# One ScalarE copy for the raw attention outputs of two groups

## What is computed

```python
# attention: 32 query heads of 16 dimensions, 8 key/value groups (4 heads each), 256 queries x 256 keys
score = einsum('bhqd,bhkd->bhqk', qh, kh) / sqrt(16)
attn  = softmax(score)
out   = einsum('bhqk,bhkd->bhqd', attn, vh)
x     = x + out @ Wfc.T + bfc
# then: layernorm, a router (2 of 8 experts), the routed experts and a shared one, added to x
```

## Time and profile before

| | |
|---|---|
| three runs | 790.33, 792.49 and 793.11 us; median 792.49 us |
| the profiled execution | 793.74 us, its span 792.0 us, granted TensorE clock 0.994 |
| attention in it | first exponential at 102.4 us, last copy of a raw result at 294.0 us |
| the even-group copies of groups 4 to 62 | first at 119.28 us, last at 289.67 us |

### The profile page before, as it was taken

The page is one execution under the profiler, slowest core; times in us unless marked ns, Lnnn a source line. Parts: engine busy times, 40 slices in busy tenths (PEclk is TensorE's granted clock), DMA queues, the critical chain, the costliest instruction groups (busy, mean ns, idle before and its releaser), DMA issues.

```text
span 792.0 us, 16078 instructions
## 1 busy us (share of the span) xinstructions
PE 760.2 (96%) x5151; PEld 406.6 (51%) x5152; DVE 576.0 (73%) x1194; ACT 429.7 (54%) x843; POOL 269.5 (34%) x224
## 2 busy tenths in 40 slices
PE   6998989999999988999999999999999999999897
PEld 4553533433433334556655656555555555555554
DVE  5767779999999966788789887555555555546767
ACT  3665579999999973455443553434343343323231
POOL 3362007999993301564300101111111111015431
PEclk9999989999999999999999999999999999999999
DMA  9997846556545788898588576877777777569985
GB/s 337 338 391 237 249 145 211 182 162 200 192 122 167 242 323 303 307 333 306 187 226 215 145 172 141 188 175 177 176 177 179 177 185 173 124 164 288 278 238 160
DMA packets 161782, 172.07 MB, mean 217 GB/s; under 512 B 103680, under 2 KB 117504, under 8 KB 161216
## 3 DMA queue, kind: packets, MB, share of 16 engines
q1 hardware_dynamic: 150012, 128.89, 55.8%
q0 software_dynamic: 11120, 41.43, 16.9%
q10 hardware_dynamic: 596, 1.07, 0.4%
HBM read 105.40 MB, written 42.73 MB: 187 GB/s over the span
## 4 chain that ended last, share of the span: by engine, by line
PE 76%; DVE 9%; DMA 7%; ACT 3%; issue 2%; SPq 2%; DVEq 0%; ACTq 0%
PE psum L1465 29%; PE psum L1477 15%; PE psum L1315 8%; PE psum L1301 6%; PE psum L1229 4%; PE psum L1401 4%; PE psum L1205 4%; DMA sb_weights<-attn_dram 3%; PE psum L1332 2%; ACT sb_weights L1025 1%; PE psum L1181 1%; DMA sb_hT<-sb_h 1%; DVE sb_weights L1747 1%; DMA sb_weights<-in_ctxT 1%; DMA sb_weights<-k_parts 1%
## 5 line engine op out<-in xcount | busy, mean ns | idle before, releaser
L1465 PE MATMUL psum<-sb_weights,sb_rows 128*128 (+1 forms) x1608 | 250.8, 313 | 0.6 <-DMA sb_rows<-xnT_dram 0.6
L1465 PEld LDWEIGHTS psum<-sb_weights,sb_rows 128*128 128x128 f16 x1608 | 157.3, 98 | 91.9 <-DMA sb_rows<-xnT_dram 1.1
L1025 ACT ACTIVATE sb_weights<-psum,sb_rows 128x512 f32<-128x512 f32 x256 | 158.6, 684 | 17.2 <-PE psum L1301 15.4
L1697 DVE TENSOR_REDUCE sb_rows<-psum 128x4 f32<-128x1024 f32 x128 | 150.1, 1214 | 6.1 <-PE psum L1229 6.1
L1477 PE MATMUL psum<-sb_weights,sb_hT 128*128 (+1 forms) x630 | 147.4, 379 | 2.5 <-DMA sb_hT<-sb_h 2.5
L894 POOL DMA_INDIRECT sb_rows<-xn_rows,sb_slot_tok x39 | 38.4, 984 | 217.9 <-DVE sb_rows L2286 147.8
L1477 PEld LDWEIGHTS psum<-sb_weights,sb_hT 128*128 128x128 f16 x630 | 61.3, 98 | 68.0 <-DMA sb_hT<-sb_h 3.7
L1301 PE MATMUL psum<-sb_weights 50*128 50x512 f16 x256 | 90.1, 391 | 3.0 <-ACT sb_weights L1025 2.6
L1094 ACT ACTIVATE psum<-psum 128x352 f32<-128x352 f32 x71 | 31.8, 448 | 112.2 <-DVE psum L1947 112.2
L1315 PE MATMUL psum<-sb_weights 128*32 128x256 f32 x1024 | 82.9, 396 | 0.0
L1229 PE MATMUL psum<-sb_weights 48*128 48x256 f16 x512 | 73.1, 275 | 1.2 <-DMA sb_weights<-k_parts 0.6
(11 more groups left out here) (264 smaller groups left out, 1013.1 us busy)
## 6 DMA issues: line engine op xcount, KB each, us to landing
sb_weights<-in_wgu SPq DMA_DIRECT2D x20, 704.0 KB, 7.8
sb_weights<-in_wgu POOLq DMA_DIRECT2D x20, 704.0 KB, 6.2
sb_weights<-in_wdn SPq DMA_DIRECT2D x17, 768.0 KB, 5.6
slot_y<-sb_rows SPq DMA_DIRECT2D x39, 256.0 KB, 2.3
sb_weights<-q_parts SPq DMA_DIRECT2D x96, 64.0 KB, 2.5
x_dram<-sb_rows SPq DMA_DIRECT2D x24, 256.0 KB, 4.4
q_parts<-sb_weights SPq DMA_DIRECT2D x16, 256.0 KB, 4.7
sb_rows<-in_x POOLq DMA_DIRECT2D x16, 256.0 KB, 4.4
```

The costliest lines, as they stand in the source:

```text
L1025: nc.scalar.activation(probs[G % 2][:, kt, pair * 512:(pair + 1) * 512], bank[4 + f % 2], ACT.Exp, scale=exp_scale[:, n:n + 1]).then_inc(e ...
L1465: mm = nc.tensor.matmul(bank[GU_BANKS[par][which]][:, 0:F], x_T[:, xp * D + k * P:xp * D + (k + 1) * P], gu(wp, k, which), start=(k == 0 a ...
L1697: nc.vector.tensor_reduce(to[:, :, j // UB, :, j % UB, qt], psum[:, banks[qt] * 512:(banks[qt] + 2) * 512] .rearrange("p (a h k) -> p a h ...
```

## The change

The pieces of `o_raw` become two of 512 columns in place of four of 256; they cover the same bytes. `pv_part` of the second batch (b = 1) writes columns 256 to 511 of bank 6, and only that of the first batch waits for a copy. `attn_out` takes a pair: one ACT instruction over the whole bank, 128 x 512, after the four exponentials of an even group, for the two groups before it. In odd groups ACT has no copy. `pv_evac` counts pairs.

```diff
-        o_raw = [rows[:, at:at + SEQ] for at in (2 * D, 2 * D + SEQ, 5 * D, 5 * D + SEQ)]
+        o_raw = [rows[:, at:at + UB * SEQ] for at in (2 * D, 5 * D)]
...
-            def attn_out(G):
+            def attn_out(p):
 
-                act.wait_ge(pv_ready, G + 1)
-                if G >= 4:
-                    act.wait_ge(ot_ready, G // 2 - 1)
-                nc.scalar.copy(o_raw[G % 4], bank[6][:, 0:SEQ]).then_inc(pv_evac, 1)
+                act.wait_ge(pv_ready, UB * (p + 1))
+                if p >= 2:
+                    act.wait_ge(ot_ready, p - 1)
+                nc.scalar.copy(o_raw[p % 2], bank[6]).then_inc(pv_evac, 1)
...
-                if G > 0:
-                    attn_out(G - 1)
-            attn_out(UNITS * UG - 1)
+                if G > 0 and G % UB == 0:
+                    attn_out(G // UB - 1)
+            attn_out(UNITS * UG // UB - 1)
...
                 pe.wait_ge(exp_done, G * FILLS + 2 * kt + 2)
-                if kt == 0 and G > 0:
-                    pe.wait_ge(pv_evac, G)
+                if kt == 0 and b == 0 and G > 0:
+                    pe.wait_ge(pv_evac, G // UB)
...
-                    mm = nc.tensor.matmul(bank[6][VW * c:VW * (c + 1), 0:SEQ], v_now,
+                    mm = nc.tensor.matmul(bank[6][VW * c:VW * (c + 1), b * SEQ:(b + 1) * SEQ], v_now,
...
             def pair_transpose(G):
 
-                pe.wait_ge(pv_evac, G + 2)
+                pe.wait_ge(pv_evac, G // UB + 1)
...
-                                                 o_raw[(G + b) % 4][:, qt * P:(qt + 1) * P], ident[:])
+                                                 o_raw[G // UB % 2][:, b * SEQ + qt * P:b * SEQ + (qt + 1) * P],
+                                                 ident[:])
```

## The result

| | before | after |
|---|---|---|
| runs beside each other | 790.33 to 794.11 us, median 792.8 (6) | 794.37 to 801.03 us, median 798.29 (6) |
| the profiled execution | 793.74 us, span 792.0, clock 0.994 | 794.37 us, span 792.6, clock 0.998 |

The changed kernel is slower, by a ratio of 1.0075 (1.0046 to 1.0105).

What follows compares the result with a forecast made beforehand. A ring of ACT and PE steps, 5.85 us a pair, was taken to bound the kernel. Copies +6.0, late keys -0.65, end +0.1 sum to +5.4 us; on the 792.49 median 797.9, stated as 798.0, range 791 to 801.

Steps and rivals of the forecast that it cites:

- The ring: Attention loop: chained ACT and PE steps take 5.85 us a pair, with the even-group copy inside and the odd-group copy outside.
- rival 1: Attention loop: PE's total work sets the pace, so the copy's growth disappears; about 792 us, chance 0.13.
- rival 2: Attention loop: ACT's total work sets the pace, so each pair saves 0.09 us; about 789.7 us, chance 0.10.
- Rival 3: Attention loop: the odd-group copy is in the ring, so its removed 0.29 us is gained; about 784 us, chance 0.06.
- The price: Even-group copy on ACT, widened to 512 columns: the next start comes 0.20 us later, bounds 0 and 0.30.
- How often: Even groups 4 to 62: 30 copies at 0.20, 6.0 us; the copy of group 2 costs nothing.
- The end: Loop's end: the last copy is 0.21 us longer, DVE busy anyway; cost at most 0.1 us, taken as 0.1.
- The late keys: PE's two waits of 0.3 us for late key loads vanish in the slower loop; -0.65 us.
- PE's wait for the wider copy: `pv_part` in even groups without the maxima's transpose may wait about 0.1 us for the copy, at no further cost.
- Everything behind moves as one block: Output projection, experts and DMAs after the loop are released by its end and only shift with it.

Runs made afterwards that it cites:

- e8: The changed kernel again, unaltered, beside the other experiments on one chip; 796.92 us against 791.75 before, 6.05 us a pair.
- e1: Changed kernel with an unused 256-column ACT copy added at the end of every odd group; 798.43 us, 1.0066 of the kernel before, 6.05 us a pair.
- e2: Changed kernel with the pair's copy cut to 256 columns; 794.88 us, 1.0058 of the kernel before, 5.85 us a pair.
- e7: Changed kernel with the pair's copy cut to 384 of 512 columns; 793.98 us in a single run, 5.94 or 5.95 us a pair.
- e11: Changed kernel, pair's transposes moved one group later into the even group, SP passing maxima on behind 8 of 12 loads; 796.46 us, 1.0062 of the kernel before.
- e3: Kernel before with PE's four transposes of a pair moved behind score fill 0; 797.58 us, 1.0057 of the kernel before, 6.07 us a pair.
- e6: Changed kernel with PE's four transposes of a pair moved ahead of score fill 3; 799.48 us, 1.0095 of the kernel before, 6.08 us a pair.
- e5: Kernel before with PE's four transposes of a pair moved ahead of score fill 3; 797.12 us, 1.0068 of the kernel before, 6.0 us a pair in the mean.
- e4: Changed kernel with PE's four transposes of a pair moved behind score fill 0; 804.23 us, 1.0141 of the kernel before, 6.28 us a pair.
- e12: Kernel before, pair's transposes moved one group later, SP passing maxima on behind 8 of 12 loads; 795.96 us, 1.0048 of the kernel before.
- e9: Changed kernel, pair's transposes moved one group later into the even group, SP passing maxima on after all key loads; 801.51 us, 1.0141 of the kernel before.

## Why the prediction was right

The forecast was 798.0 us, measured were 798.29; +5.4 against the median, measured +5.5 and, in e8, +5.2. The mechanism held. That the size agrees to 0.1 us is partly luck: the interval of the ratio is +3.6 to +8.3 us, and one term was 0.55 us off. Step by step:

- **The ring, and which copy is in it.** Held. e1 shows the odd copy outside, e2 and e7 the even copy inside, e11 that it leaves the ring when the transposes change places. PE alone (rival 1) and ACT's total work (rival 2) both kept the pace at 5.85 or below; it went to 6.05. Rival 3 would have given 5.56.
- **Rival 2, ACT's total work**, pointed the wrong way: ACT's busy time fell by 2.1 us in the loop and the kernel became slower. By the rule of the Trainium skill that stood beside it ("Perfetto Trace Analysis", *Identifying the Most-Contended Engine*) the change would have helped; the trace doesn't agree (ACT 154.86 us busy in place of 156.99, and the stretch 5.67 us longer).
- **The price, 0.20 us a copy.** Held: 0.49 to the next start against 0.29. A pair grew from 5.85 to 6.05 us. The Trainium skill ("ScalarE: Activation LUTs", *What ACT_TABLE_LOAD costs*) would have made it 0.213, 6.4 in the sum. The copy itself grew by that much, from 372 to 586 ns; the distance to the next start, which is what counts, grew by 0.20.
- **How often.** 29 pairs from group 4 to 62 became 0.20 longer, 5.8 us, and the last even-group copy is the thirtieth: from its start to the output projection's first transposes it is 298.77 - 292.18 = 6.59 us, before 296.05 - 289.67 = 6.38. The copy of group 2, sized at nothing, cost 0.06: from it to the copy of group 4 it is 116.12 - 109.43 = 6.69 us, before 119.28 - 112.65 = 6.63.
- **The end.** Sized at 0.1, and about right: from the last copy's start to the output projection it is 2.17 us, before 2.07. From group 62's copy to the last one it is 4.42 us (292.18 to 296.60), before 4.31: 0.11 longer and not 0.20. The prediction gave nothing for waits of PE that go; here one did count. Before, the last group's `pv_part` started at 292.85, behind an odd-group copy that ended at 292.71; after, it starts right behind the transposes. So the 0.21 of this stretch is 0.20 for group 62's copy, 0.10 for the last copy, and 0.10 won back.
- **The late keys.** This step was wrong: "both waits should vanish" (-0.65). One did, the other grew to 0.53 us: its load landed 3.6 us after its issue, where the median is 2.1. Measured in the loop: -0.1 (5.8 - 0.1 = 5.7, the stretch's 5.67). In e8 0.2 was left, so the term differs from one execution to the next.
- **PE's wait for the wider copy.** Expected at about 0.1 in pairs without the transpose of the maxima, measured 0.2, 16 times, and as expected without a price.
- **"Everything behind moves as one block".** The profiled pair doesn't show it, since the stretch behind was 2.1 us shorter. That a slower loop doesn't shorten it is argued in the last section from the other profiles and from the totals.

The miss of the study lies in its expectations of e3 to e6. The ring of before was right, but I worked out the new rings from PE's visible waits as if they were free time. PE's work had hidden overlap in its order: in e5 and e6 the transposes broke it, and in e3 and e4 they stood ahead of fills that ACT then waited for.

## What to carry to other kernels

Merging two instructions saves fixed cost, but it moves work in time: ask which of the two stood in the ring that sets the pace, and whether the merged one stands there too. Close the ring by hand, from one instruction round to its next copy, and check it in a stretch where one engine has less work and the period stays. e5 is the counterexample: without the `max_fill`s its period fell from 6.0 to 5.69, so there PE's work was in the ring. Compare loops by their period in the profile; two profiles 0.6 us apart hid a change of 5.

## What the runs showed of the hardware

The times follow the mean granted clock of each execution: over 181 runs of all these kernels (77 of the one before), a straight line common to them, with a level for each kernel, gives 0.66 us for each 0.001 of mean granted clock (standard error 0.06). At the same clock the changed kernel is 6.1 us (0.5 standard error) over the one before, e1 6.0, e2 2.2, e11 3.6 and e12 2.4. For e2 some 0.7 of it are late keys in its profile; the rest of it, 1.5 us with an error of 0.7, and of e12 is open.

A part of e2's lower clock is seen in its profile, at the start of the output projection. PE in e2 and before:

```profile
294.40 1.56 PE L1396 MATMUL psum<-sb_ident,sb_weights 128*128 128x128 f32 x8 [1.24 <-DVE sb_rows L1829]
295.87 4.88 PE L1404 MATMUL psum<-sb_weights 128*128 128x512 f32 x8
```

```profile
296.05 1.09 PE L1393 MATMUL psum<-sb_ident,sb_weights 128*128 128x128 f32 x8 [0.99 <-DVE sb_rows L1826]
297.46 3.70 PE L1401 MATMUL psum<-sb_weights 128*128 128x512 f32 x8 [0.31 <-ACT sb_weights L1035]
```

In e2 the granted clock was 0.72 over these first 6 us, behind an idle time of 1.24 us, and the work took 6.35 us; before it was 1.00, behind 0.99 us, and 5.11 us. The same drop (0.72 to 0.75) stands in the profiles of e4 to e6 and e9 to e12, and in none of after, e1, e3, e7 and e8. It lowers the mean clock, so the line above has already taken it off, and what is open stays open.

Three profiles with 6.05 us a pair (after, e1, e8) took 493.5 to 493.9 us from the output projection's first transposes to the end, those of before, e2 and e7 496.0 to 497.0. That the slower loop gives some 2 us back there is unlikely: e3, with 6.07 us a pair, took 499.0, and the changed kernel's 6.1 us in total at the same clock are the loop's 5.9. One profile of each kernel doesn't settle what the differences are.
